# Softplus sum moved to TensorE, five GpSimd readouts and a reordered step-product store in a two-layer selective-scan kernel

## The chip, the cores and the metric

One core of a Trainium2 chip runs the whole program in one launch. The metric is device time in microseconds, median of several runs; lower is better. Engines are named TensorE (PE), VectorE (DVE), ScalarE (ACT), GpSimd (POOL) and SyncE (SP, which issues the DMAs).

## The reference

Two layers, each a selective scan ("mamba") followed by a mixture of experts. The change touches only the scan. For each of 4 sequences of 2305 positions:

```python
u = silu(conv4(u) + conv_b)                       # u, z = in_proj(seq)
dt = softplus(dt_raw @ dt_proj_w.T + dt_proj_b)
A = -exp(A_log)                                   # 128 channels x 16 states
def step(h, (dt_t, B_t, C_t, u_t)):
    dA = exp(dt_t[:, :, None] * A)
    h = dA * h + (dt_t * u_t)[:, :, None] * B_t[:, None, :]
    return h, einsum('bdn,bn->bd', h, C_t)
y = (ys + u * D) * silu(z)
out = y @ out_proj_w.T
```

## The kernel before, in words

A sequence is cut into 5 chunks of TC = 462 positions, so a layer runs NCH = 20 chunks one after the other, and the program runs 40. The 128 x 16 channel-state pairs make ITEMS = 16 tiles of 128 partitions, the items 0 to 15 of a chunk. For an item:

- GpSimd makes `dbu` (L689), the product of a row of dt times u and a row of B, in 4 buffers;
- ScalarE makes the decay exp(dt A) (L621) into one of 5 PSUM banks `state`;
- VectorE scans (`tensor_tensor_scan`). For items in ON_DVE the result stays in the bank (L811) and VectorE multiplies it by C into `hc` (L797), two neighbours in one instruction where it can; L795 copies the last column to `carry`. For items in ON_POOL the scan writes `last` (L808) and GpSimd multiplies it by C into `hcp` (L684). These multiplications are the readouts;
- TensorE sums the readouts into `ysum` with selection matrices (L504, L509).

A bank can be refilled when its scan (ON_POOL) or its readout (ON_DVE) is done. VectorE gates chunk k-1's sum with silu(z) (`gate`, L775) after item 2 of chunk k.

Beside the items of chunk k runs the front of chunk k+2: TensorE projects u, z (L446 to L451), then dt and B, C (L456, L460) into two PSUM banks `front`; ScalarE takes Silu (L550, L551), then for softplus Abs, Relu, Exp (L557 to L560), 1+e (L564), Ln (L568). `prep_rr` on VectorE (L714) makes a rounding remainder `rr`, `prep_ln` (L720) subtracts it from the Ln, `prep_dt` (L726) adds the Relu part and gives dt in `dd`. GpSimd's `prep` (L649) makes dt times u, here called the step product. SyncE stores B, C (`store_bc`, L338) and dt, dt times u (`store_dt`, four DMAs, L344) to DRAM and loads them back replicated over partitions into `rep` (`replicate_bc`, L351; `replicate_dt`, L359; four DMAs of 462 KB each). `rep` has two halves, one for each parity of chunks. Chunk k waits on `rep_loaded` for its half.

SyncE, like every engine, runs its list in order; in the loop of chunk k it holds: replicate_bc(k+1), store_dt(k+1), replicate_dt(k+1), load_xs(k+3), store_bc(k+2). The first of these waits for the last readout of chunk k-1. The front of chunks 0 and 1 is made ahead of the loop, between the tiles of the input's normalisation; here it is called the prologue.

Of the kernel before, what the change touches and what calls it, by code (L numbers as in the profile page):

```python
# [14 lines left out]
ALU = mybir.AluOpType  # L15
# [28 lines left out]
ON_POOL = (0, 3, 6, 8, 11, 13)  # L44
# [202 lines left out]
def phase_mamba(nc, a, g, l):  # L247
# [4 lines left out]
    with ExitStack() as ctx:  # L252
# [3 lines left out]
        u, sz = sb("u", [P, UBUFS, TC]), sb("sz", [P, UBUFS, TC])  # L256
        ab, ex, rx, rr = sb("ab", [P, TC]), sb("ex", [P, TC]), sb("rx", [P, TC]), sb("rr", [P, TC])
# [21 lines left out]
        xs_loaded, rep_loaded, bc_stored, dt_stored = sem("xs_loaded"), sem("rep_loaded"), sem("bc_stored"), sem("dt_stored")  # L279
# [28 lines left out]
        RESTS = NCH - 3 + (3 if l == 0 else 0)  # L308
# [3 lines left out]
        def chunk_of(eng, tile, k):  # L312

            if isinstance(k, int):
                return tile[:, k % UBUFS, :]
            return tile[:, bass.ds(eng.snap(k % UBUFS), 1), :]

        @block.sync
        def _(sp):
# [119 lines left out]
        def _(pe):  # L439
# [10 lines left out]
            def prep_z(k):  # L450
# [1356 lines left out]
```

## Time and profile before

| | before |
|---|---|
| median of 3 runs | 1935.14 us (1932.81 to 1940.75) |
| profiled execution | 1938.45 us, of which the span on the core is 1936.7 us |
| busy in the span | PE 1546.9, DVE 1271.6, POOL 1211.5, ACT 991.2 us |

The profile counts an engine busy while an instruction of its own runs; neighbouring instructions overlap by about 0.1 us, so the distance from one start to the next is what an instruction costs. Idle time is put down to the releaser whose event came last. Times in rows are microseconds from the start of the span.

### The profile page before, as it was taken

Reading aid. Unit: us, or ns where it says so; the run is one execution under the profiler, and the core shown is the slowest. Engines: PE = TensorE matmul, PEld = TensorE weight load, DVE = VectorE, ACT = ScalarE, POOL = GpSimd, SP = SyncE. Lnnn points to the kernel's source line nnn. Section 1 sums busy time; section 2 is a strip of 40 time slices with the busy share of each in tenths; the row PEclk is TensorE's granted clock in tenths of the full one; section 3 lists DMA queues with packets and bytes.
Section 4 is the critical chain, followed back from the end, with each engine's and each line's share of the span. In section 5 each row is a group of like instructions: output and inputs, shape, how many; then the busy total and the mean of one; then the engine's idle time right before and its main releaser. Section 6 shows DMA issues by size and latency. Waiting matters only on the chain. (4 is left out here: it accounts for less than half of the span.)

```text
span 1936.7 us, 25492 instructions
## 1 busy us (share of the span) xinstructions
PE 1546.9 (80%) x6220; PEld 927.2 (48%) x6221; DVE 1271.6 (66%) x2146; ACT 991.2 (51%) x1594; POOL 1211.5 (63%) x1179
## 2 busy tenths in 40 slices
PE   5677777777778998999982687777777777699996
PEld 3222222222228998989981222222222227566664
DVE  5799999999996531111115799999999996411012
ACT  4777777777772211222223777777777772122112
POOL 2699999999981001444435699999999992123310
PEclk8799999999995899999995799999999995599997
DMA  5788777787774204777765877788877881423313
GB/s 131 191 183 185 181 179 177 176 186 179 178 160 155 85 25 143 233 220 218 226 162 134 206 179 176 179 182 179 181 176 174 184 186 49 171 78 122 123 62 107
DMA packets 104507, 311.06 MB, mean 161 GB/s; under 512 B 19389, under 2 KB 74509, under 8 KB 93069
## 3 DMA queue, kind: packets, MB, share of 16 engines
q1 hardware_dynamic: 91896, 291.72, 60.1%
q0 software_dynamic: 12544, 18.63, 4.1%
q8 instruction: 20, 0.33, 0.1%
q14 instruction: 47, 0.38, 0.1%
HBM read 258.83 MB, written 51.45 MB: 160 GB/s over the span
## 5 line engine op out<-in xcount | busy, mean ns | idle before, releaser
L689 POOL TENSOR_TENSOR mamba_dbu<-mamba_rep 128x462 f32<-128x462 f32 x640 | 677.2, 1085 | 66.1 <-DMA mamba_rep<-dt_rows 66.1
L509 PE MATMUL mamba_ysum<-mamba_hc,all_sel 128*128 128x462 f32 x800 | 379.4, 588 | 148.3 <-DVE mamba_hc L797 147.3
L621 ACT ACTIVATE mamba_state<-mamba_rep,all_m_acol 128x462 f32<-128x462 f32 x640 | 388.9, 638 | 156.6 <-DVE mamba_last L808 155.6
L811 DVE TENSOR_TENSOR_SCAN mamba_state<-mamba_state,mamba_carry,mamba_dbu 128x462 f32<-128x462 f32 x400 | 455.4, 1179 | 0.0
L509 PEld LDWEIGHTS mamba_ysum<-mamba_hc,all_sel 128*128 128x128 f32 x800 | 130.3, 190 | 398.3 <-DVE mamba_hc L797 318.8
L808 DVE TENSOR_TENSOR_SCAN mamba_last<-mamba_state,mamba_last,mamba_dbu 128x462 f32<-128x462 f32 x240 | 280.3, 1168 | 15.2 <-POOL mamba_dbu L689 12.4
L684 POOL TENSOR_TENSOR mamba_hcp<-mamba_last,mamba_rep 128x462 f32<-128x462 f32 x240 | 266.7, 1111 | 5.6 <-DVE mamba_last L808 5.6
L504 PE MATMUL mamba_ysum<-mamba_hcp,all_sel 128*128 128x462 f32 x480 | 227.8, 570 | 50.1 <-POOL mamba_hcp L684 50.0
L797 DVE TENSOR_TENSOR mamba_hc<-mamba_state,mamba_rep 128x462 f32<-128x462 f32 (+1 forms) x240 | 230.7, 961 | 0.0
L1433 DVE TENSOR_TENSOR moe_h<-moe_sg,moe_up 128x512 f32<-128x512 f32 x62 | 42.6, 688 | 283.0 <-PE moe_up L1242 276.6
L504 PEld LDWEIGHTS mamba_ysum<-mamba_hcp,all_sel 128*128 128x128 f32 x480 | 85.3, 190 | 172.4 <-POOL mamba_hcp L684 119.6
L621 ACT ACT_TABLE_LOAD x80 | 102.6, 1283 | 103.6 <-DMA mamba_rep<-dt_rows 102.7
L1203 POOL DMA_INDIRECT token_rows<-moe_eo,moe_row x44 | 69.8, 1586 | 133.4 <-ACT moe_eo L1376 122.8
L1188 POOL DMA_INDIRECT moe_xs<-normed_rows,moe_row x44 | 43.5, 989 | 150.8 <-DVEq L1524 82.6
L1682 POOL DMA_INDIRECT last_rows<-experts_eo,all_row x32 | 31.5, 984 | 152.5 <-DVE experts_eo L1657 152.5
L1633 ACT ACTIVATE experts_hT<-experts_hid,weights_b 128x432 f32<-128x432 f32 x64 | 39.6, 620 | 156.0 <-PE experts_hid L1607 151.4
L1284 PE MATMUL moe_down<-weights_wd,moe_h 128*128 (+1 forms) x496 | 117.4, 380 | 0.8 <-ACT moe_eo L1376 0.8
L1616 PE MATMUL experts_down<-weights_w,experts_hT 128*108 128x256 f32 x512 | 112.5, 380 | 1.3 <-ACT experts_hT L1633 0.7
L1616 PEld LDWEIGHTS experts_down<-weights_w,experts_hT 128*108 128x108 f32 x512 | 87.9, 173 | 24.5 <-ACT experts_hT L1633 1.9
L1607 PE MATMUL experts_hid<-experts_xT,weights_w 128*128 128x432 f32 x256 | 96.3, 535 | 1.1 <-issue 1.1
L1284 PEld LDWEIGHTS moe_down<-weights_wd,moe_h 128*128 128x128 f32 x496 | 89.5, 190 | 10.8 <-issue 1.2
L1376 ACT ACTIVATE moe_eo<-moe_down,moe_weight 128x256 f32<-128x256 f32 x44 | 20.8, 473 | 135.7 <-PE moe_down L1284 135.7
(236 smaller groups left out, 2285.6 us busy)
## 6 DMA issues: line engine op xcount, KB each, us to landing
mamba_rep<-bc_rows SPq DMA_DIRECT2D x168, 462.0 KB, 7.4
mamba_rep<-dt_rows SPq DMA_DIRECT2D x168, 462.0 KB, 7.5
weights_wgu<-in_L_gu_dram SPq DMA_DIRECT2D x88, 512.0 KB
dt_rows<-mamba_dd SPq DMA_DIRECT2D x168, 115.5 KB, 7.2
weights_w<-in_L_w_dram SPq DMA_DIRECT2D x16, 1024.0 KB
mamba_xs<-seq_scratch SPq DMA_DIRECT2D x92, 116.0 KB, 9.2
seq_scratch<-mamba_y SPq DMA_DIRECT2D x40, 116.2 KB, 7.0
normed_rows<-xn SPq DMA_DIRECT2D x16, 288.0 KB, 7.1
```

Source lines behind the costliest of these rows:

```text
L504: nc.tensor.matmul(ysum[:, 0:TC], sel[:, i // NM, :], hcp[:, n % HCP, :], start=False, stop=end).then_inc(hcp_summed, 1)
L509: nc.tensor.matmul(ysum[:, 0:TC], sel[:, i // NM, :], hc[:, n % HCD, :], start=False, stop=end).then_inc(hc_summed, 1)
L621: nc.scalar.activation(state[:, STATE_BANK[i], 0:TC], rep[:, par * REP_ROWS + i // NM, :], ACT.Exp, scale=m["acol"][:, i:i + 1]).then_inc( ...
L684: pool.tensor_tensor(hcp[:, n % HCP, :], last[:, n, :], rep[:, first + 3 * NG + i % NM, :], ALU.mult).then_inc(hcp_ready, 1)
L689: pool.tensor_tensor(dbu[:, i % 4, :], rep[:, first + NG + i // NM, :], rep[:, first + 2 * NG + i % NM, :], ALU.mult).then_inc(dbu_ready, 1)
L797: nc.vector.tensor_tensor(hc[:, n % HCD:n % HCD + width, :], state[:, bank:bank + width, 0:TC], rep[:, c_rows + i % NM:c_rows + i % NM + w ...
L808: nc.vector.tensor_tensor_scan(last[:, n, :], bank, dbu[:, i % 4, :], last[:, n, TC - 1:TC], ALU.mult, ALU.add).then_inc(scan_done, 1)
L811: nc.vector.tensor_tensor_scan(bank, bank, dbu[:, i % 4, :], carry[:, i:i + 1], ALU.mult, ALU.add).then_inc(scan_done, 1)
L1203: pool.indirect_dma_start(out=g["to"][r % 2][:, :], out_offset=bass.IndirectOffsetOnAxis(ap=row[:, r:r + 1], axis=0), in_=eo[:, r % 2, :], ...
L1284: mm = nc.tensor.matmul(down[:, 0:C], h[:, par, f * P:(f + 1) * P], weights, start=(f == 0), stop=(f == FC0 - 1), skip_group_check=True)
L1607: mm = nc.tensor.matmul(hid[:, f % 2, 0:CAP], w1[:, par, k, f * P:(f + 1) * P], xT[:, par, k, :], start=(k == 0), stop=(k == 1))
L1616: mm = nc.tensor.matmul(down[0:CT, i % 2, 0:C], hT[:, f, i * CT:(i + 1) * CT], w2[:, par, f, :], start=(f == 0), stop=(f == FC1 - 1))
```

## The change

- `prep_ln` and `prep_dt` leave VectorE. ScalarE's Ln goes to `ab` in SBUF; TensorE adds `ab` + `rx` - `rr` with three matmuls (identity, identity, and `nident`, its negative) into the second `front` bank (`prep_add`); ScalarE copies the sum to `dd` (`prep_dd`).
- ON_POOL has five items, not six: (1, 4, 7, 10, 13). VectorE reads out eleven. Items 11 and 12 take C rows 3 and 0 and can't share an instruction. `hcp` has 5 buffers, `hc` 7.
- ScalarE's Silu for chunk k+2 stands behind decay 3 (it stood behind decay 6), Ln behind decay 12 (it stood behind 15), the new copy behind decay 15.
- GpSimd's step product for k+2 stands at the end of chunk k; it stood behind dbu 3 of chunk k+1.
- TensorE projects u and z one chunk earlier, for k+3 inside chunk k, and z waits for all of ScalarE's work on k+2. In SyncE's list store_dt(k+2) stands ahead of the wait for that z. `dt_rows` has two halves.
- `replicate_dt` counts on a semaphore of its own, `step_loaded`: ScalarE waits on it alone, VectorE on `rep_loaded` alone, GpSimd on both.
- The loops of SyncE, TensorE and ScalarE are written out, where they were loops with a register.

```diff
-ON_POOL = (0, 3, 6, 8, 11, 13)
+ON_POOL = (1, 4, 7, 10, 13)
-HCP = 3
-HCD = 5
-AT_SILU, AT_EXP, AT_ONE, AT_LN, AT_BC, AT_DT, AT_DTU, AT_Y, AT_RR = 6, 10, 11, 15, 13, 3, 3, 2, 13
+HCP = 5
+HC_SLOT = (0, 1, 2, 3, 4, 5, 6, 1, 2, 3, 4)
+AT_SILU, AT_EXP, AT_ONE, AT_BC, AT_LN, AT_U, AT_DTU, AT_Y, AT_RR, AT_ADD, AT_DD = 3, 6, 7, 8, 12, 9, 1, 2, 8, 7, 15
...
-            with sp.Fori(0, NCH) as k:
+            for k in range(NCH):
                 sp.wait_ge(decay_ready, items_before)
                 sp.wait_ge(dbu_ready, items_before)
+                sp.wait_ge(rep_loaded, replicas_before)
+                sp.wait_ge(step_loaded, replicas_before)
+                replicate_dt(k + 1)
                 sp.wait_ge(hc_ready, START + ND * k)
                 sp.wait_ge(hcp_ready, START + NP_ * k)
-                sp.wait_ge(rep_loaded, replicas_before)
                 replicate_bc(k + 1)
-                store_dt(k + 1)
-                replicate_dt(k + 1)
-                sp.wait_ge(front_mm, START + MMS * (k + 2) + MM_Z)
-                load_xs(k + 3)
                 store_bc(k + 2)
+                store_dt(k + 2)
+                sp.wait_ge(front_mm, START + MMS * (k + 3) + MM_Z)
+                load_xs(k + 4)
...
             def prep_z(k):
+                pe.wait_ge(front_act, START + ACTS * k)
...
+            def prep_add(k):
+                pe.wait_ge(front_act, START + ACTS * k + A_LN)
+                nc.tensor.matmul(front[:, 1, 0:TC], g["ident"][:, :], ab[:, :], start=True, stop=False)
+                nc.tensor.matmul(front[:, 1, 0:TC], g["ident"][:, :], rx[:, :], start=False, stop=False)
+                pe.wait_ge(front_dve, START + DVES * k + D_R)
+                nc.tensor.matmul(front[:, 1, 0:TC], nident[:, :], rr[:, :], start=False, stop=True).then_inc(front_mm, 1)
...
                 if s == AT_U1:
+                    pe.wait_ge(minus_ready, 1)
+                    prep_add(0)
                     prep_u(1)
                     prep_z(1)
...
-            def prep_ln(k):
-                nc.vector.tensor_tensor(front[:, 1, 0:TC], front[:, 1, 0:TC], rr[:, :], ALU.subtract).then_inc(front_dve, 1)
-            def prep_dt(k):
-                nc.vector.tensor_tensor(dd[:, 0, :], front[:, 1, 0:TC], rx[:, :], ALU.add).then_inc(front_dve, 1)
+            def prep_dd(k):
+                act.wait_ge(front_mm, START + MMS * k + MM_ADD)
+                nc.scalar.activation(dd[:, 0, :], front[:, 1, 0:TC], ACT.Copy).then_inc(front_act, 1)
```

Three places show how instructions move. The first is VectorE across the end of a chunk and the start of the next, before; `mamba_last` is what the scan of an ON_POOL item writes, `mamba_state` the PSUM banks.

```order
L811 SCALAR_TENSOR_TENSOR mamba_state<-mamba_state,mamba_carry,mamba_dbu 128x462 [waits mamba0_dbu_ready,mamba0_decay_ready] x2
L720 TENSOR_TENSOR mamba_front<-mamba_front,mamba_rr 128x462 [waits mamba0_front_dve,mamba0_front_act]
L795 COPY mamba_carry<-mamba_state 128x2 [waits mamba0_scan_done]
L797 TENSOR_TENSOR mamba_hc<-mamba_state,mamba_rep 128x924 [waits mamba0_hc_summed]
L726 TENSOR_TENSOR mamba_dd<-mamba_front,mamba_rx 128x462 [waits mamba0_front_dve,mamba0_dt_stored]
L808 SCALAR_TENSOR_TENSOR mamba_last<-mamba_state,mamba_last,mamba_dbu 128x462 [waits mamba0_dbu_ready,mamba0_decay_ready,mamba0_hcp_ready,mamba0_rep_loaded,mamba0_carry_zeroed]
```

The same place in the changed kernel, from the readout of items 11 and 12 to the scan of item 4 of the next chunk:

```order
L798 TENSOR_TENSOR mamba_hc<-mamba_state,mamba_rep 128x462
L813 SCALAR_TENSOR_TENSOR mamba_state<-mamba_state,mamba_carry,mamba_dbu 128x462 [waits mamba0_dbu_ready,mamba0_decay_ready] x2
L794 COPY mamba_carry<-mamba_state 128x2 [waits mamba0_scan_done]
L798 TENSOR_TENSOR mamba_hc<-mamba_state,mamba_rep 128x924 [waits mamba0_hc_summed]
L813 SCALAR_TENSOR_TENSOR mamba_state<-mamba_state,mamba_carry,mamba_dbu 128x462 [waits mamba0_decay_ready,mamba0_dbu_ready,mamba0_rep_loaded,mamba0_carry_zeroed]
L810 SCALAR_TENSOR_TENSOR mamba_last<-mamba_state,mamba_last,mamba_dbu 128x462 [waits mamba0_hcp_ready,mamba0_dbu_ready,mamba0_decay_ready]
L794 COPY mamba_carry<-mamba_state 128x1 [waits mamba0_scan_done]
L798 TENSOR_TENSOR mamba_hc<-mamba_state,mamba_rep 128x462 [waits mamba0_hc_summed]
L813 SCALAR_TENSOR_TENSOR mamba_state<-mamba_state,mamba_carry,mamba_dbu 128x462 [waits mamba0_dbu_ready,mamba0_decay_ready]
L774 TENSOR_TENSOR mamba_y<-mamba_ysum,mamba_sz 128x462 [waits mamba0_hcp_summed,mamba0_hc_summed]
L813 SCALAR_TENSOR_TENSOR mamba_state<-mamba_state,mamba_carry,mamba_dbu 128x462 [waits mamba0_dbu_ready,mamba0_decay_ready]
L810 SCALAR_TENSOR_TENSOR mamba_last<-mamba_state,mamba_last,mamba_dbu 128x462 [waits mamba0_hcp_ready,mamba0_dbu_ready,mamba0_decay_ready]
```

L720 and L726 are gone, and the carry copy that waits for the last scan stands right behind it, with nothing between.

The second is ScalarE over the first five decays of a chunk, in the changed kernel (before, the Silu pair stood behind the seventh):

```order
L630 ACTIVATE mamba_state<-mamba_rep,all_m_acol 128x462 [waits mamba0_hc_ready,mamba0_step_loaded]
L630 ACTIVATE mamba_state<-mamba_rep,all_m_acol 128x462 [waits mamba0_scan_done]
L630 ACTIVATE mamba_state<-mamba_rep,all_m_acol 128x462 [waits mamba0_hc_ready] x2
L551 ACT_TABLE_LOAD [waits mamba0_y_ready]
L551 ACTIVATE mamba_u<-mamba_front,all_m_vec 128x462 [waits mamba0_front_mm]
L552 ACTIVATE mamba_sz<-mamba_front 128x462
L630 ACT_TABLE_LOAD
L630 ACTIVATE mamba_state<-mamba_rep,all_m_acol 128x462 [waits mamba0_scan_done]
```

Decays 2 and 3 take the banks that items 14 and 15 of the chunk before held, and two table loads and both Silus now stand between decay 3 and decay 4.

The third is SyncE in one chunk of the changed kernel:

```order
L352 DMA mamba_rep<-dt_rows 32x3696 [waits mamba0_step_loaded,mamba0_rep_loaded,mamba0_dt_stored,mamba0_dbu_ready,mamba0_decay_ready]
L352 DMA mamba_rep<-dt_rows 32x3696 x3
L344 DMA mamba_rep<-bc_rows 32x3696 [waits mamba0_bc_stored,mamba0_hcp_ready,mamba0_hc_ready]
L344 DMA mamba_rep<-bc_rows 32x3696 x3
L330 DMA bc_rows<-mamba_bc 32x462 [waits mamba0_front_act]
L337 DMA dt_rows<-mamba_dd 64x1x462 [waits mamba0_front_pool]
L337 DMA dt_rows<-mamba_dd 64x1x462 x3
L322 DMA mamba_xs<-seq_scratch 64x464 [waits mamba0_front_mm]
L322 DMA mamba_xs<-seq_scratch 64x464
```

Both replications now follow each other, and the stores of the next step product come last but one.

## Rows read from the trace of the kernel before

**Rows 1.** Windows, gate to gate: length, busy (instructions) PE PEld DVE ACT POOL, clock, DMA, GB/s.

```profile
73.30:554.90 481.60, 372.76 (x835) 139.57 (x836) 475.06 (x615) 357.56 (x532) 457.39 (x437) 1.00 0.79 180
1095.80:1579.00 483.20, 373.82 (x836) 139.93 (x836) 474.73 (x615) 357.56 (x532) 457.10 (x437) 0.99 0.80 179
```

**Rows 2.** Waits in the first of these windows: total us, times, longest.

```profile
DVE mamba_last L808 <- POOL mamba_dbu L689: 4.8, 10, 0.8
...
POOL mamba_dbu L689 <- DMA mamba_rep<-dt_rows: 23.7, 19, 2.5
```

**Rows 3.** Timeline of VectorE in one chunk: start, length, instruction.

```profile
335.08 1.16 DVE L808 TENSOR_TENSOR_SCAN mamba_last<-mamba_state,mamba_last,mamba_dbu 128x462 f32<-128x462 f32 x1
336.15 0.14 DVE L795 COPY mamba_carry<-mamba_state 128x1 f32<-128x1 f32 x1
336.20 0.64 DVE L797 TENSOR_TENSOR mamba_hc<-mamba_state,mamba_rep 128x462 f32<-128x462 f32 x1
336.75 2.26 DVE L811 TENSOR_TENSOR_SCAN mamba_state<-mamba_state,mamba_carry,mamba_dbu 128x462 f32<-128x462 f32 x2
...
346.50 0.64 DVE L720 TENSOR_TENSOR mamba_front<-mamba_front,mamba_rr 128x462 f32<-128x462 f32 x1
347.03 0.17 DVE L795 COPY mamba_carry<-mamba_state 128x2 f32<-128x2 f32 x1
347.10 1.12 DVE L797 TENSOR_TENSOR mamba_hc<-mamba_state,mamba_rep 128x924 f32<-128x924 f32 x1
348.13 0.65 DVE L726 TENSOR_TENSOR mamba_dd<-mamba_front,mamba_rx 128x462 f32<-128x462 f32 x1
348.74 1.18 DVE L808 TENSOR_TENSOR_SCAN mamba_last<-mamba_state,mamba_last,mamba_dbu 128x462 f32<-128x462 f32 x1
...
351.97 0.62 DVE L775 TENSOR_TENSOR mamba_y<-mamba_ysum,mamba_sz 128x462 f32<-128x462 f32 x1
352.51 1.17 DVE L808 TENSOR_TENSOR_SCAN mamba_last<-mamba_state,mamba_last,mamba_dbu 128x462 f32<-128x462 f32 x1
```

**Rows 4.** Timeline of VectorE in the prologue: the second needs the first's result.

```profile
60.10 0.65 DVE L720 TENSOR_TENSOR mamba_front<-mamba_front,mamba_rr 128x462 f32<-128x462 f32 x1
60.85 0.64 DVE L726 TENSOR_TENSOR mamba_dd<-mamba_front,mamba_rx 128x462 f32<-128x462 f32 x1
```

**Rows 5.** Timeline of ScalarE: from Silu's table load to the next decays; two decays.

```profile
329.41 1.28 ACT L550 ACT_TABLE_LOAD   x1
...
333.10 2.36 ACT L621 ACTIVATE mamba_state<-mamba_rep,all_m_acol 128x462 f32<-128x462 f32 x4
...
341.18 1.22 ACT L621 ACTIVATE mamba_state<-mamba_rep,all_m_acol 128x462 f32<-128x462 f32 x2
```

**Rows 6.** Timeline of TensorE in a chunk: projections, two records to a matmul.

```profile
349.93 0.94 PE L446 MATMUL mamba_front<-mamba_xs,all_m_wu 128*128 128x462 f32 x2
350.71 0.94 PE L447 MATMUL mamba_front<-mamba_xs,all_m_wu 128*128 128x462 f32 x2
```

**Rows 7.** DMA issues of SyncE in one chunk.

```profile
351.94 2.59 SPq L344 DMA_DIRECT2D dt_rows<-mamba_dd  x4
360.84 1.72 SPq L359 DMA_DIRECT2D mamba_rep<-dt_rows  x4
```

**Rows 8.** Us to landing (last number): a store behind replicas; a store alone.

```profile
dt_rows<-mamba_dd SPq DMA_DIRECT2D x1, 115.5 KB, 6.8
...
seq_scratch<-mamba_y SPq DMA_DIRECT2D x1, 116.2 KB, 2.4
```

**Rows 9.** Timelines of the prologues: TensorE, then VectorE in layer 0 and layer 1.

```profile
43.62 1.75 PE L447 MATMUL mamba_front<-mamba_xs,all_m_wu 128*128 128x462 f32 x2
45.16 1.75 PE L451 MATMUL mamba_front<-mamba_xs,all_m_wz 128*128 128x462 f32 x2
...
70.08 1.18 DVE L808 TENSOR_TENSOR_SCAN mamba_last<-mamba_state,mamba_last,mamba_dbu 128x462 f32<-128x462 f32 x1
...
1091.35 0.44 DVE L777 MEMSET mamba_ysum<- 128x462 f32 x1 [10.64 <-DMA seq_scratch<-mamba_y]
```

More of the change, by code:

```diff
@@ L54 @@
 SUM_ORDER = tuple(sorted(range(ITEMS), key=lambda i: LAST_OF[i] + 2 if i in ON_DVE else i + 3.1))
-HCP = 3
-HCD = 5
-AT_SILU, AT_EXP, AT_ONE, AT_LN, AT_BC, AT_DT, AT_DTU, AT_Y, AT_RR = 6, 10, 11, 15, 13, 3, 3, 2, 13
+HCP = 5
+HC_SLOT = (0, 1, 2, 3, 4, 5, 6, 1, 2, 3, 4)
+HC_GAP = tuple(min(d for d in range(1, ND + 1) if HC_SLOT[n - d] == HC_SLOT[n]) for n in range(ND))
+HCD = max(HC_SLOT) + 1
+AT_SILU, AT_EXP, AT_ONE, AT_BC, AT_LN, AT_U, AT_DTU, AT_Y, AT_RR, AT_ADD, AT_DD = 3, 6, 7, 8, 12, 9, 1, 2, 8, 7, 15
 START = 16
@@ L372, in _ @@
                 sp.wait_ge(zeroed, 1)
-                for k in range(NCH, NCH + 3):
+                for k in range(NCH, NCH + 4):
                     sp.dma_start(g["seq"][k], hc[0:DM, :, :].rearrange("p n c -> p (n c)")[:, 0:CW]).then_inc(seq_rest, 16)
-            replicas = sp.alloc_register(f"replicas{l}")
             sp.wait_ge(padded, 3)
@@ L403, in _ @@
                     store_seq(b, c)
+            store_dt(1)
             sp.wait_ge(seq_rest, 16 * RESTS)
+            sp.wait_ge(front_mm, START + MMS * 2 + MM_Z)
+            load_xs(3)
             tiles["room_free"](sp)
-            with sp.Fori(0, NCH) as k:
-                sp.reg_mul(replicas, k, 16 * REPS)
-                sp.reg_add(replicas, replicas, 16 * REPS)
-                replicas_before = sp.snap(replicas)
+            for k in range(NCH):
+                replicas_before = 16 * NS * (k + 1)
                 items_before = START + ITEMS * k
@@ L492, in _ @@
                 tiles["tensor_weights"](pe, 1)
-            with pe.Fori(0, NCH) as k:
-                prep_u(k + 2)
-                prep_z(k + 2)
+            prep_add(1)
+            prep_u(2)
+            prep_z(2)
+            for k in range(NCH):
+                prep_dt(k + 2)
+                prep_bc(k + 2)
                 pe.wait_ge(y_ready, START + k)
-                nc.tensor.matmul(ysum[:, 0:TC], m["diag"][:, :], chunk_of(pe, u, k), start=True, stop=False)
+                nc.tensor.matmul(ysum[:, 0:TC], m["diag"][:, :], chunk_of(u, k), start=True, stop=False)
                 for at, i in enumerate(SUM_ORDER):
@@ L508, in _ @@
                         pe.wait_ge(hc_ready, START + ND * k + n + 1)
-                        nc.tensor.matmul(ysum[:, 0:TC], sel[:, i // NM, :], hc[:, n % HCD, :],
+                        nc.tensor.matmul(ysum[:, 0:TC], sel[:, i // NM, :], hc[:, HC_SLOT[n], :],
                                          start=False, stop=end).then_inc(hc_summed, 1)
-                    if at == AT_DT:
-                        prep_dt(k + 2)
-                    if at == AT_DT + 1:
-                        prep_bc(k + 2)
+                    if at == AT_ADD:
+                        prep_add(k + 2)
+                    if at == AT_U:
+                        prep_u(k + 3)
+                        prep_z(k + 3)
             pe.wait_ge(front_dve, START + DVES * (NCH + 2))
@@ L607, in _ @@
             nc.scalar.preload_act_table_set("exp_and_others")
-            with act.Fori(0, NCH // 2) as pair:
+            for pair in range(NCH // 2):
                 for par in range(2):
                     k = pair * 2 + par
-                    act.wait_ge(rep_loaded, 16 * REPS * (k + 1))
+                    act.wait_ge(step_loaded, 16 * NS * (k + 1))
                     for i in range(ITEMS):
```

106 lines of the change are left out of this document (49 added, 57 removed).

## The prediction

> **What bounds the kernel now.** I read three views in this order: the windows over each layer's chunks, who waits for whom inside them, and the timeline of one chunk. The windows show what fills a chunk. From the gate of chunk 0 to that of chunk 19 are 19 chunks: 481.6 / 19 = 25.35 us a chunk in layer 0 and 483.2 / 19 = 25.43 in layer 1, mean 25.39 [rows 1]. VectorE is busy 475.06 / 19 = 25.00 us of it, GpSimd 24.07, TensorE 19.62, ScalarE 18.82 [rows 1]. VectorE is the bound with 0.34 to 0.45 us idle a chunk. The waits say why it idles: 4.8 us in 19 chunks are for GpSimd's dbu, and GpSimd itself sat 23.7 us in 19 waits, 1.25 us each, for the replicas of dt [rows 2]. So there is a second loop just short of the bound: last readout, replicate_bc, store_dt, replicate_dt, first dbu. 40 of these chunks are some 1015 us of 1936.7. TensorE's granted clock there is 1.00 and 0.99 [rows 1], the level of 2.4 GHz.
>
> **VectorE's own work in a chunk** (start to start). Leaving: L720, 347.03 - 346.50 = 0.53, and L726, 348.74 - 348.13 = 0.61 [rows 3]. Coming: one more readout. Of eleven, 8 go in 4 double instructions as now, 3 go single (item 0, and 11 and 12 apart) where now 2 do, so one single of 336.75 - 336.20 = 0.55 [rows 3]. Six carry copies stay six; a scan into a bank and one into `last` both cost some 1.08. Work: 25.00 - 1.14 + 0.55 = 24.41 us.
>
> **What VectorE newly waits for.** First, the carry copy of items 14 and 15 now comes right behind the scan that it needs. Before, L720 stood between. An independent successor starts 0.09 us before its predecessor ends (335.08 + 1.16 against 336.15) [rows 3]; L726, which needed L720, began 0.10 after its end (60.10 + 0.65 against 60.85) [rows 4]. That is up to 0.19; other such pairs are not in my rows, and I take 0.16, with 0 to 0.25 as bounds.
> Second, decay 4. Count from the start of the readout of 14 and 15. It is over at 1.12 [rows 3] and frees the banks of decays 2 and 3. ScalarE then needs 1.22 for the two, 333.10 - 329.41 = 3.69 from Silu's table load to the next decay, and 2.36 / 4, about 0.64 with its tail, for decay 4 [rows 5]. With 0.07 for two hand-offs (an estimate; the bounds are 0 and the 0.10 of [rows 4] twice) it is ready at 6.75. VectorE would begin scan 4 at 1.03 (readout) + 4 x 1.08 (scans 0 to 3) + 0.05 + 0.55 (readout 0) + 0.54 (gate, 352.51 - 351.97) = 6.49 [rows 3]. It waits 0.26 to 0.30, every chunk; I take 0.29. Before, Silu came three decays later and had cover. Bounds: 0, if decay 2 gets away earlier, and 0.6.
> Third, what is left of today's idle: 0.07 (the sequence starts). The wait for GpSimd, 4.8 / 19 = 0.25 in layer 0 [rows 2], goes, if the next parts hold.
> New chunk: 24.41 + 0.16 + 0.29 + 0.07 = 24.93 us, against 25.39: 0.46 less, times 40 = 18 us.
>
> **GpSimd.** It does 22 multiplications, not 23, at 24.07 / 23 = 1.05 us [rows 1]: 23.0 us. Its readout of item 13 can begin 3.4 us before the last double readout (scans 14 and 15, one copy, the two singles lie between), the step product follows, so dbu 0 of the next chunk is done 0.2 us before the origin above, needed at 1.03. Cover 1.2 us.
>
> **TensorE.** 3 more matmuls at 350.71 - 349.93 = 0.78 [rows 6]: 19.6 + 2.3 = 22 us of 24.9. They hide in its waits for readouts. Ln ends near 16.4 us (decay 12 follows the readout of 5 and 6, then two table loads), the sum is there at 19.0, ScalarE copies by 20.1, behind decay 15 at 19.5; then z goes. Behind z's wait are queued the sums of items 10 to 15, which end at about 3.0 of the next chunk, the gate wants them at 4.9. Cover 1.9 us; without it each us late is a us a chunk. ScalarE gains one copy of about 0.55 and is at 19.4 of 24.9.
>
> **DMA and SyncE.** The step product now ends at -1.2 us. Four stores are issued in 2.6 us [rows 7], the last lands 2.4 us after its issue if nothing lies ahead, 6.8 behind replicas [rows 8]. The queue is empty there, so I take 2.4: SyncE, which has issued load_xs meanwhile, can replicate dt at 3.4, and behind it B and C. DMA work is 0.79 x 25.35 = 20.0 us a chunk [rows 1]; by bytes (8 x 462 KB of 8 x 462 + 4 x 115.5 + 2 x 116 + 58) the eight replicas are 16.7 of it. With 2.4 for start and landing and 0.3 for a bc store they are in at 22.8; VectorE loses nothing up to 24.9. Cover 2.1 us. The bc replication, today behind the last readout and first in the list, moves past dt's; both have the half free by then.
> The Trainium skill, DMA: Bandwidth & Descriptors, on the path of one DMA, puts most of a fixed cost of about 2 us on the write receipt and says that it "can cause a surprisingly long delay especially when the write target is HBM". The lone store agrees with its usual figure; its long case is the fourth rival.
>
> **The prologues**, which the change lengthens. Outside the loop nothing hides the addition: TensorE runs there at 45.16 - 43.62 = 1.54 us a matmul, half speed [rows 9], so three cost 4.6. Layer 0: the first addition delays the remaining tiles by 4.6, less about 1.7 since VectorE no longer stops there for Ln (an estimate; 0 to 2.3): 2.9. The second stands ahead of ScalarE's last weights: 4.6 + 0.55 for the copy - 1.28 for a table load that falls away with the loop - 1.0 that ScalarE has in hand today: 2.9. The first scan moves from 70.08 [rows 9] to about 75.9: 5.8 us. Layer 1: the first scan hangs on the stored sequence with VectorE idle 10.64 us until 1091.35 [rows 9], so much of the same 2.9 + 2.9 is covered; I take 2 (0 to 5). Together 7.8 (4 to 11).
> Behind the loop two of the saved VectorE instructions lie in its wait for the last sum: nothing.
>
> **Sum.** 1938.45 - 18.4 + 7.8 = 1927.9 for the profiled execution. That one lies 0.17% above the median of 1935.14, so 1925 as a median.
>
> **Rivals**, as medians.
> 1. The forecast, 1915 to 1935: chance 0.48.
> 2. The two new waits are not there (decay 2 starts early enough, a dependent copy is free): another 0.45 x 40 = 18 us, 1907. For it: ScalarE is idle over 6 us a chunk. Against: decay 2's bank is the one just read. 0.15.
> 3. ScalarE or TensorE later than counted: the chain Ln, sum, copy, z, item 10 has five hand-offs, and Silu with its loads has none to spare. A further 0.25 us a chunk gives 1935. 0.17.
> 4. The opposite side: the stores. If their landing takes 6.8 us without a queue too, the replicas are in at 22.8 + 4.4 = 27.2, 2.3 late. A step product made in chunk k feeds chunk k+2, so that is paid once in two chunks: 1.15 a chunk, 24.93 + 1.15 = 26.1, 40 x 0.7 = 28 slower, and the prologue: about 1970. It decides from 2.4 + 2.1 = 4.5 us on; halfway beyond it the time is some 1945. Against it: the lone store. 0.10.
> 5. The change doesn't do what it says: VectorE stays at 25.4, since it meets GpSimd or the code, now three times as long on TensorE, is late; only the prologue shows, 1943. 0.10.
>
> **From cases to numbers.** What differs by less than 0.5%, 9.7 us, this measurement hardly tells from no change; that bound is 1925.5 and the forecast sits on it. Faster: all of 2, somewhat over half of 1, a little of 3: 0.46. Same: the rest of 1, 3 and most of 5: 0.38. Slower: 4 and part of 5: 0.16. The range runs from 1908, at the edge of case 2, to 1946, which takes in 3, 5 and the near half of 4; case 1 alone is 1915 to 1935.
>
> **What would show it.** Gate to gate 24.9 us; VectorE busy 24.4 to 24.5; a wait of VectorE for decay 4 of near 0.3 in every chunk; no wait of GpSimd or ScalarE for replicas; last dt store landed in under 3 us; first scans near 76 and 1095. Wrong if GpSimd still waits for bc replicas (case 4), if the gate waits for `ysum` (case 3), or if the first scans come as early as before.

## The result, and the profile after

The changed kernel takes 1925.49 us (median of 5 runs, 1922.10 to 1929.57) against 1939.33 for the kernel before (median of 5 runs beside it; the 3 runs known at the time of the prediction gave 1935.14): ratio 0.9941, interval 0.9922 to 0.9959. The forecast was 1925.0. Beside the experiments the kernel before was timed again, with medians of 1940.12 (e1 to e4), 1939.66 (e5 to e8) and 1934.67 (e9 to e12), so kernels of different groups are compared by ratio. The profiled execution took 1925.49 us, its span 1923.7.

Windows of the kernel after, gate of chunk 0 to gate of chunk 19, layer 0 and layer 1, to be read against [rows 1]:

```profile
77.00:549.10 472.10, 400.65 (x951) 168.83 (x951) 468.12 (x597) 367.23 (x553) 432.43 (x419) 0.98 0.84 183
1093.30:1565.00 471.70, 400.62 (x950) 168.53 (x949) 468.07 (x597) 365.98 (x552) 432.82 (x419) 0.98 0.85 184
```

A chunk takes 472.1 / 19 = 24.85 and 24.83 us, where it took 25.35 and 25.43. Each layer's first gate is later on its own clock, though: 77.0 against 73.3 in layer 0, and in layer 1 the gate stands 53.8 us behind the first load of x, against 50.8. Of both, 0.6 us is the place of the gate and no delay: the readout of item 0 now stands ahead of it (3.85 us from the first scan to the gate in layer 0, 3.24 before). For the second, SyncE's issue of that load, before and after, and the gates' 1095.80 and 1093.30 of the windows:

```profile
1045.05 1.12 SPq L323 DMA_DIRECT2D mamba_xs<-seq_scratch  x2
```

```profile
1039.55 1.10 SPq L322 DMA_DIRECT2D mamba_xs<-seq_scratch  x2
```

Waits inside the first window, against [rows 2]. VectorE's wait for GpSimd and GpSimd's for the replicas of dt are gone; a wait for a decay is new:

```profile
DVE mamba_last L810 <- ACT mamba_state L630: 3.2, 16, 0.3
...
POOL mamba_dbu L702 <- DMA mamba_rep<-bc_rows: 1.0, 2, 0.8
```

VectorE in one chunk, against [rows 3]. The carry copy begins after the end of the scans (343.13 + 2.24 = 345.37), and the scan of item 4 waits 0.18 us for its decay:

```profile
343.13 2.24 DVE L813 TENSOR_TENSOR_SCAN mamba_state<-mamba_state,mamba_carry,mamba_dbu 128x462 f32<-128x462 f32 x2
345.41 0.16 DVE L794 COPY mamba_carry<-mamba_state 128x2 f32<-128x2 f32 x1
...
352.26 1.18 DVE L810 TENSOR_TENSOR_SCAN mamba_last<-mamba_state,mamba_last,mamba_dbu 128x462 f32<-128x462 f32 x1 [0.18 <-ACT mamba_state L630]
```

The DMA part of the page (last number: us to landing). A step store lands in 2.3 us, the lone store's 2.4 of [rows 8]; before it was 7.2:

```profile
dt_rows<-mamba_dd SPq DMA_DIRECT2D x176, 115.5 KB, 2.3
```

### The profile page after: what moved, and what is told of

The parts are those of the page before. It is cut to its first block and busy times, and to the rows that moved or that the text cites. A ratio compares the mean times of both kernels' runs of the same rounds, so it can differ in the third digit from the quotient of the medians.

```text
span 1923.7 us, 22854 instructions
## 1 busy us (share of the span) xinstructions
PE 1617.1 (84%) x6496; PEld 995.0 (52%) x6497; DVE 1250.0 (65%) x2100; ACT 1012.7 (53%) x1637; POOL 1158.8 (60%) x1141
## 5 line engine op out<-in xcount | busy, mean ns | idle before, releaser
L813 DVE TENSOR_TENSOR_SCAN mamba_state<-mamba_state,mamba_carry,mamba_dbu 128x462 f32<-128x462 f32 x440 | 504.8, 1172 | 0.7 <-ACT mamba_state L630 0.4
L517 PE MATMUL mamba_ysum<-mamba_hc,all_sel 128*128 128x462 f32 x880 | 392.4, 565 | 55.1 <-DVE mamba_hc L798 54.1
L517 PEld LDWEIGHTS mamba_ysum<-mamba_hc,all_sel 128*128 128x128 f32 x880 | 159.9, 191 | 261.1 <-issue 133.5
L798 DVE TENSOR_TENSOR mamba_hc<-mamba_state,mamba_rep 128x924 f32<-128x924 f32 (+1 forms) x280 | 250.0, 905 | 0.0
L810 DVE TENSOR_TENSOR_SCAN mamba_last<-mamba_state,mamba_last,mamba_dbu 128x462 f32<-128x462 f32 x200 | 231.6, 1158 | 6.4 <-ACT mamba_state L630 6.3
L697 POOL TENSOR_TENSOR mamba_hcp<-mamba_last,mamba_rep 128x462 f32<-128x462 f32 x200 | 200.8, 1004 | 40.7 <-DVE mamba_last L810 39.2
L512 PE MATMUL mamba_ysum<-mamba_hcp,all_sel 128*128 128x462 f32 x400 | 187.7, 551 | 0.0
L512 PEld LDWEIGHTS mamba_ysum<-mamba_hcp,all_sel 128*128 128x128 f32 x400 | 76.2, 190 | 80.0 <-issue 79.5
L453 PE MATMUL mamba_front<-mamba_u,all_m_wdt 128*128 128x462 f32 x88 | 49.1, 642 | 80.3 <-ACT mamba_sz L552 80.3
L1616 PEld LDWEIGHTS experts_down<-weights_w,experts_hT 128*108 128x108 f32 x512 | 87.9, 173 | 24.5 <-ACT experts_hT L1633 1.9
```

What stands on the lines that cost most here:

```text
L512: nc.tensor.matmul(ysum[:, 0:TC], sel[:, i // NM, :], hcp[:, n % HCP, :], start=False, stop=end).then_inc(hcp_summed, 1)
L517: nc.tensor.matmul(ysum[:, 0:TC], sel[:, i // NM, :], hc[:, HC_SLOT[n], :], start=False, stop=end).then_inc(hc_summed, 1)
L697: pool.tensor_tensor(hcp[:, n % HCP, :], last[:, n, :], rep[:, first + 3 * NG + i % NM, :], ALU.mult).then_inc(hcp_ready, 1)
L798: nc.vector.tensor_tensor(hc[:, HC_SLOT[n + w]:HC_SLOT[n + w] + at_once, :], state[:, bank + w:bank + w + at_once, 0:TC], rep[:, c_rows + ...
L810: nc.vector.tensor_tensor_scan(last[:, n, :], bank, dbu[:, i % 4, :], last[:, n, TC - 1:TC], ALU.mult, ALU.add).then_inc(scan_done, 1)
L813: nc.vector.tensor_tensor_scan(bank, bank, dbu[:, i % 4, :], carry[:, i:i + 1], ALU.mult, ALU.add).then_inc(scan_done, 1)
```

## Experiments

Twelve kernels, each profiled and timed against the kernel before. "Chunk" is gate 0 to gate 19 over 19, in layer 0 and layer 1. The stretch between the two layers' chunks, where most instructions are the same in all of them, differs from one profiled execution to the next (462 to 473 us), so mechanisms are read from chunks and gates, and time from ratios.

| kernel | chunk, us | ratio, interval |
|---|---|---|
| before | 25.35, 25.43 | 1 |
| after | 24.85, 24.83 | 0.9941 (0.9922 to 0.9959) |
| e1 old SyncE order | 25.02, 25.16 | 1.0002 (0.9990 to 1.0014) |
| e2 one matmul | 24.82, 24.82 | 0.9922 (0.9909 to 0.9935) |
| e3 Silu later | 24.57, 24.57 | 0.9898 (0.9884 to 0.9912) |
| e4 sum on VectorE | 25.93, 25.92 | 1.0128 (1.0111 to 1.0145) |
| e5 e3 + readout later | 24.45, 24.44 | 0.9862 (0.9840 to 0.9884) |
| e6 six readouts | 24.52, 24.53 | 0.9864 (0.9844 to 0.9885) |
| e7 prologue sum on VectorE | 24.83, 24.84 | 0.9924 (0.9907 to 0.9940) |
| e8 before, loops written out | 25.10, 25.16 | 0.9953 (0.9936 to 0.9970) |
| e9 e7 + store later | 24.83, 24.85 | 0.9932 (0.9919 to 0.9946) |
| e10 e5 + e9 | 24.43, 24.44 | 0.9860 (0.9843 to 0.9878) |
| e11 e6 + e9 + readout later | 24.46, 24.44 | 0.9873 (0.9854 to 0.9891) |
| e12 before, SyncE's loop written out | 25.07, 25.07 | 0.9943 (0.9927 to 0.9959) |

### e1: the old SyncE order in the kernel after

```diff
-                replicate_dt(k + 1)
                 sp.wait_ge(hc_ready, START + ND * k)
                 sp.wait_ge(hcp_ready, START + NP_ * k)
                 replicate_bc(k + 1)
-                store_bc(k + 2)
-                store_dt(k + 2)
+                if k > 0:
+                    store_dt(k + 1)
+                replicate_dt(k + 1)
                 sp.wait_ge(front_mm, START + MMS * (k + 3) + MM_Z)
                 load_xs(k + 4)
+                store_bc(k + 2)
+            store_dt(NCH + 1)
```

> The kernel after, with SyncE's issues in a chunk put back as they were: replicas of b and c, then the step stores, then the step replicas, then z's wait and the load of x, then the store of b and c. My theory: the stores queue behind the 14 us replicas again and land in about 7 us instead of 2.3, but the step replicas still end some 1.6 us before they are needed (2.1 before the change, less the 0.5 us by which a chunk is shorter), so the loops stay at 24.85 us a chunk and the time at 1925, within 4. Rival: the DMA chain binds, VectorE and ScalarE wait for step replicas at each chunk's start by 0.2 to 0.4 us: 1933 to 1941.

Measured 1.0002: the whole gain in time is gone. The rival holds and my expectation was wrong, by a plain error: 2.1 us is the cover that the prediction worked out for the new order. The old one had none, since GpSimd waited 1.25 us a chunk in it [rows 2]. Timeline of ScalarE, its wait at the head of a chunk, and the page's landing of the step stores:

```profile
346.01 2.38 ACT L632 ACTIVATE mamba_state<-mamba_rep,all_m_acol 128x462 f32<-128x462 f32 x4 [4.77 <-DMA mamba_rep<-dt_rows]
```

```profile
dt_rows<-mamba_dd SPq DMA_DIRECT2D x176, 115.5 KB, 8.7
```

And its windows:

```profile
75.20:550.60 475.40, 406.19 (x951) 170.70 (x952) 468.15 (x597) 367.01 (x553) 429.23 (x418) 0.97 0.80 182
1099.70:1577.80 478.10, 406.83 (x950) 171.12 (x950) 467.71 (x597) 365.00 (x551) 428.99 (x418) 0.97 0.80 181
```

VectorE is busy 24.6 us a chunk as in the kernel after, yet the chunk stays at 25.0 to 25.2. That this is the period of SyncE's loop of stores and replicas is borne out by e12, where the order is the same, VectorE has its old work of 25.0 us, and the chunk is 25.07. With the old order in place, VectorE's saving turns into waiting, here for dbu, as GpSimd and ScalarE stand still at the head of a chunk (23.9 and 87.7 us in 19 chunks, ScalarE's for the replicas of dt):

```profile
DVE mamba_state L815 <- POOL mamba_dbu L704: 5.0, 10, 1.2
```

So 0.30 of the 0.55 us that the change takes off a chunk stays in e1, as much as the written-out loop brings alone in e12, and 0.25 goes. Against the kernel after, the longer chunks explain some 10 of the 12 us (0.61%) that e1 is slower. Against the kernel before, the chunks of both layers save 11 us in the profile, the longer prologues take back 3.7, and stretches that the edits don't touch are 7.9 longer; no run shows why.

### e2: one matmul for the sum

```diff
-                nc.tensor.matmul(front[:, 1, 0:TC], g["ident"][:, :], ab[:, :], start=True, stop=False)
-                nc.tensor.matmul(front[:, 1, 0:TC], g["ident"][:, :], rx[:, :], start=False, stop=False)
                 pe.wait_ge(front_dve, START + DVES * k + D_R)
-                nc.tensor.matmul(front[:, 1, 0:TC], nident[:, :], rr[:, :], start=False, stop=True).then_inc(front_mm, 1)
+                nc.tensor.matmul(front[:, 1, 0:TC], g["ident"][:, :], ab[:, :], start=True, stop=True).then_inc(front_mm, 1)
```

> The kernel after, with one matmul in place of the three in TensorE's sum: the ReLU part and the polynomial part are left out of the step size, so the output isn't the reference's. My theory: the three matmuls are free in the loops, where TensorE waits 1.8 us a chunk for Silu, and cost only on the dependent chain of the prologues: 2 matmuls less, three times at the slow 1.5 us in the first layer's prologue and at about 0.8 us in the second's; so 2 to 5 us less, 1922, and a chunk unchanged at 24.84. Rival: TensorE's position sets the step chain or the readout slots: 0.1 to 0.3 us off each chunk, 1914 to 1921, with the chunk at 24.55 to 24.75.

The chunk stays at 24.82: inside the loops the two matmuls that e2 leaves out are free. The third and ScalarE's copy were not tried alone. Layer 0's first gate comes at 74.6 and not 77.0, the 2 us expected of the prologue, but with the same prologue it came at 75.4 in e3 and 77.9 in e5, and the ratios' intervals overlap: what the two matmuls cost there isn't shown.

### e3: Silu and Exp one decay later

```diff
-AT_SILU, AT_EXP, AT_ONE, AT_BC, AT_LN, AT_U, AT_DTU, AT_Y, AT_RR, AT_ADD, AT_DD = 3, 6, 7, 8, 12, 9, 1, 2, 8, 7, 15
+AT_SILU, AT_EXP, AT_ONE, AT_BC, AT_LN, AT_U, AT_DTU, AT_Y, AT_RR, AT_ADD, AT_DD = 4, 7, 8, 9, 12, 9, 1, 2, 8, 7, 15
```

> The kernel after, with ScalarE's two Silus behind decay 4 instead of 3 and the Exp group behind decay 7 instead of 6. My theory: VectorE's wait of 0.18 us for decay 4 with the 0.10 us of lost overlap goes, and no other decay comes late, because the Exp group moves too: 0.28 us off each of 40 chunks, 11 us, 1914 (1911 to 1918). Rival: ScalarE is late by the same at the next decay that it does after a table load (decay 5 or 8), or TensorE, held 1.2 us longer at the Silu wait, gives back the readout slots late: 1925, 1923 to 1929.

24.84 - 24.57 = 0.27 us a chunk (expected: 0.28), and VectorE has no wait for a decay left. Four numbers in a list bring three quarters as much as the whole change (0.9898 against 0.9941). The 11 us appear as 0.43%, some 8 us, in the ratios, whose intervals allow both.

### e4: the sum back on VectorE

In part; the rest takes out TensorE's three matmuls and ScalarE's copy and does the same to the prologues:

```diff
...
+                        if i == 11:
+                            prep_ln(k + 2)
                         if i - 1 in ON_DVE and not FIRST[i - 1]:
                             read_out(i - 2 if SECOND[i - 1] else i - 1)
+                        if i == 13:
+                            prep_dt(k + 2)
...
```

> The kernel after, with the sum of the softplus parts back on VectorE as two additions behind scans 11 and 13 of a chunk (and in the prologues), and TensorE's three matmuls and ScalarE's copy taken out. Everything else stays, the store order and the five GpSimd readouts too. My theory: VectorE is the bound and has no hidden room, so each chunk grows by the two additions, 2 x 0.55 us = 1.1, so 24.84 to 25.95, 44 us in all, and the prologues give 3 to 6 us back: 1965 (1960 to 1971). Rival: ScalarE's and GpSimd's waits share the bound, so part of the additions hides in the 0.2 us idle and the 0.3 us of late decay 4: +0.6 to 0.8 a chunk, 1944 to 1952.

Measured 1966.6, the chunk 25.93: +1.08, both additions in full. Windows of layer 0:

```profile
76.10:568.70 492.60, 371.66 (x833) 153.82 (x833) 488.96 (x634) 355.53 (x530) 437.95 (x418) 0.95 0.81 175
```

VectorE's busy time grew by (488.96 - 468.12) / 19 = 1.10. So with the store order in, VectorE is the bound; e1 says that without it, it isn't.

### e5: the carry copy away from its scan

On top of e3's edit:

```diff
-                        if i - 1 in ON_DVE and not FIRST[i - 1]:
+                        if i - 1 in ON_DVE and not FIRST[i - 1] and i != 13:
                             read_out(i - 2 if SECOND[i - 1] else i - 1)
+                    read_out(11)
```

> The kernel of the later Silu (chunk 24.50 us, 1919.5), with one more move: the double readout of items 11 and 12 goes from behind scan 13 to behind scan 15, between that scan and the carry copy of items 14 and 15, which needs scan 15's result. My theory: the copy's exposed dependency of 0.13 us a chunk goes, 5 us in all: 24.37 us a chunk, 1914. Rival: ScalarE's decay 0, which writes the bank that this readout frees, starts 2.3 us later, and VectorE waits for it at the chunk's start, 0.1 to 0.5 us: 1918 to 1935.

24.57 - 24.44 = 0.13 a chunk and 1913.36 us. Both terms for which the prediction had new waits are now priced by themselves, and without them the windows give

```profile
77.90:542.40 464.50, 406.36 (x950) 174.75 (x950) 463.85 (x597) 364.35 (x552) 430.80 (x418) 0.95 0.85 186
```

24.45 us a chunk with VectorE idle for 0.03: the prediction's bare work was 24.41.

### e6: six readouts on GpSimd

```diff
-ON_POOL = (1, 4, 7, 10, 13)
+ON_POOL = (0, 3, 6, 8, 11, 13)
...
-HCP = 5
-HC_SLOT = (0, 1, 2, 3, 4, 5, 6, 1, 2, 3, 4)
+HCP = 3
+HC_SLOT = (0, 1, 2, 3, 4, 5, 6, 0, 1, 2)
```

> The kernel after, with six readouts on GpSimd at the items of the kernel before and ten on VectorE; the sum on TensorE and the store order stay. My theory: VectorE loses one single readout of 0.55 us and GpSimd comes to 22.8 + 1.0 = 23.8 us of a chunk, not yet the bound; some of the 0.55 is lost to waits for GpSimd, so 24.85 falls to 24.45, 16 us less, 1910 (1904 to 1918). Rival: GpSimd, without cover, takes its place as the bound together with the handing back of scans, at 24.8 us or more: 1925 to 1935.

```profile
74.70:540.60 465.90, 396.40 (x950) 168.39 (x950) 458.98 (x577) 367.33 (x552) 458.33 (x437) 0.99 0.85 186
```

24.52 a chunk and ratio 0.9864: going from six readouts to five, which the change does, costs 0.3 us a chunk with the rest in place. GpSimd (458.33 / 19 = 24.12) and VectorE (24.16) are then level. The 0.3 is the price of the whole list of items and not of a readout alone, since the scans' order and VectorE's waits for decays change with it (3.2 us in 16 waits in the kernel after, 2.4 in 10 here).

### e7 and e9: the prologues

e7 puts the sums of chunks 0 and 1 on VectorE; e9 has this edit besides:

```diff
-            store_dt(1)
             sp.wait_ge(seq_rest, 16 * RESTS)
+            store_dt(1)
```

> The kernel after, with the sum for chunks 0 and 1 alone, outside the loops, back on VectorE; the loops keep TensorE's. My theory: the two groups of three matmuls at half clock with their copies leave the prologues' chain: the first scan of the first layer goes from 73.1 to about 69.5 us, that of the second gains 1 to 3 us: 5 us less in all, 1920 (1917 to 1923). Rival: VectorE again stops for Ln in the first prologue and the second hangs on the stored sequence: 1 us or less, 1925.

> The kernel of the VectorE sum in the prologues, with the prologue's second group of step stores moved behind SyncE's wait for the stored sequence. In that run VectorE's first instruction after the prologue waited until 71.15 us for the sequence, 7.4 us after its last store was issued, against 4.6 us in the kernel before, and four step stores stood right behind it in the queue. My theory: those stores slow the sequence's landing. Moved, the sequence lands some 2.5 us sooner, the first scan of layer 0 begins at 69.5 to 70.5 and not at 72.3, and layer 1's likewise 2 us sooner: 1920 to 1921. Rival: the landing varies by itself or the replicas are the cause, the first scan stays at 72, 1925.

Timelines of SyncE and VectorE, e7, then e9. The first instruction behind the prologue waits for the sequence in both:

```profile
57.21 6.50 SPq L359 DMA_DIRECT2D seq_scratch<-mamba_y  x10
63.76 3.49 SPq L337 DMA_DIRECT2D dt_rows<-mamba_dd  x4
...
71.15 0.44 DVE L787 MEMSET mamba_ysum<- 128x462 f32 x1 [6.70 <-DMA seq_scratch<-mamba_y]
```

```profile
57.09 7.92 SPq L359 DMA_DIRECT2D seq_scratch<-mamba_y  x10
69.18 2.51 SPq L337 DMA_DIRECT2D dt_rows<-mamba_dd  x4
...
69.42 0.44 DVE L787 MEMSET mamba_ysum<- 128x462 f32 x1 [2.31 <-DMA seq_scratch<-mamba_y]
```

With four step stores right behind it, the sequence was in 71.15 - 63.71 = 7.4 us after its last issue, without them 69.42 - 65.01 = 4.4. The first scan began at 72.34 and 70.61, just outside the range of the theory. This is weaker than it looks. e9's last issue came 1.3 us later by itself; and e10, which has e9's order and nothing behind the sequence, took 6.7 us from the last issue. Counted from the first of the ten issues, the sequence took 13.9 us in e7 and 14.7 in e4, which both have step stores right behind it, and 11.9 to 13.2 in the six kernels without (before, e8 to e12); e2, with the stores 2 us behind, is between them at 13.7. The means differ by 1.7 us, so the theory is likely in layer 0, at less than the expected 2.5 us, and not shown by one pair of executions. In layer 1 nothing moved (47.9 and 47.8 us from the first load of x to that instruction), where I expected 2 us. By ratio e7, e9 and the kernel after can't be told apart, so the prologue's microseconds are seen in the profile alone.

### e8 and e12: the kernel before with loops written out

```diff
-            with sp.Fori(0, NCH) as k:
-                sp.reg_mul(replicas, k, 16 * REPS)
-                sp.reg_add(replicas, replicas, 16 * REPS)
-                replicas_before = sp.snap(replicas)
+            for k in range(NCH):
+                replicas_before = 16 * REPS * (k + 1)
```

That is e12; e8 does the same to TensorE's and ScalarE's loops too.

> The kernel before, with the loops of SyncE, TensorE and ScalarE over the chunks written out and nothing else changed. My theory: registers and branches lie in waits, so nothing but the table load behind the loop's head changes: 1939, within 3 (chunk 25.39). Rival: the loops' registers sit on the chain of SyncE's replicas that VectorE meets, and 0.1 to 0.3 us a chunk comes back: 1927 to 1935; or longer code fetches cost the same the other way, 1943 to 1950.

> The kernel before, with SyncE's loop over the chunks alone written out. With all three loops written out a chunk went from 25.28 to 25.03 us and the time to 1929.6. SyncE then issued the first replica of b and c 0.14 us after the readout that frees the rows, against 0.67 us in loop form. My theory: that half microsecond sits on the loop of stores and replicas that GpSimd waited for, so SyncE's loop gives most of it: chunk 25.03 to 25.12, 1930 to 1934. Rival: the gain is from TensorE's or ScalarE's loop (ScalarE's wait for the replicas at the chunk's head fell from 2.7 to 1.1 us): chunk 25.25, 1939.

For e8 I expected nothing and was wrong; e12's theory holds. e12's chunk is 25.07, 0.32 less than before, its ratio 0.9943, that of the whole change. Windows and waits of e12 in layer 0:

```profile
72.90:549.20 476.30, 372.51 (x836) 139.71 (x836) 474.59 (x615) 357.66 (x532) 457.25 (x437) 1.00 0.81 181
```

```profile
POOL mamba_dbu L687 <- DMA mamba_rep<-dt_rows: 18.5, 18, 2.1
...
DVE mamba_last L806 <- POOL mamba_dbu L687: 0.8, 2, 0.5
```

VectorE's work is untouched (474.59 / 19 = 24.98), its wait for GpSimd is down from 4.8 to 0.8 us [rows 2]. The half microsecond is seen at SyncE. In the kernel before, the readout that frees the rows ends at 372.07 + 1.12 = 373.19 and the replicas are issued 0.58 us later; in e12 it is 368.62 + 1.13 = 369.75 and 0.14. In 18 chunks of layer 0 it is 0.56 to 0.58 before and 0.13 to 0.15 in e12. The profile doesn't show the register instructions themselves; that they are the cause follows from the edit, which changes nothing else. First before, then e12:

```profile
372.07 1.12 DVE L797 TENSOR_TENSOR mamba_hc<-mamba_state,mamba_rep 128x924 f32<-128x924 f32 x1
...
373.77 1.96 SPq L351 DMA_DIRECT2D mamba_rep<-bc_rows  x4
```

```profile
368.62 1.13 DVE L795 TENSOR_TENSOR mamba_hc<-mamba_state,mamba_rep 128x924 f32<-128x924 f32 x1
...
369.89 1.70 SPq L351 DMA_DIRECT2D mamba_rep<-bc_rows  x4
```

e8's chunk is 25.10 and 25.16, so TensorE's and ScalarE's loops add nothing to this.

### e10 and e11: together

e10 is e5 with both prologue edits; e11 is e6 with them and with item 12's readout behind scan 15.

> The later Silu and Exp groups, the readout of 11 and 12 behind scan 15, the prologues' sum on VectorE and their second step stores behind the wait for the sequence, all on the kernel after. My theory: the gains lie in different places and add: chunk 24.38 as with the first two (1913.4), and 5 us of prologues: 1909 (1905 to 1913). Rival: the prologue part gives nothing, as in its first form: 1913.

> Six readouts on GpSimd (chunk 24.51, 1914.3), with the single readout of item 12 behind scan 15 and the two prologue edits, Silu where the change has it. GpSimd is busy 24.1 us of that chunk and VectorE 24.15. My theory: GpSimd is now level with VectorE, so of the 0.13 us dependency some 0.05 to 0.1 comes back: chunk 24.43, and 5 us of prologues, 1906 (1902 to 1911). Rival: GpSimd binds, the chunk stays at 24.5, and only the prologues show: 1909; or decay 0 is late and costs 0.2 a chunk, 1917.

Both chunks came out as expected (24.44 and 24.45). The time, 1906.4 and 1911.34 us beside 1934.67, is no better by ratio than e5's and e6's. The intervals of e5, e6, e10 and e11 overlap, so none of them is shown to be the best: they are 1.3 to 1.4% below the kernel before and 0.7 to 0.8% below the change. The 5 us that were expected of the prologues don't show in the ratios.

## Why the prediction was right, and where it was not

**The bound.** That VectorE was the bound with a second loop just behind it was right, and both halves matter: e4 shows the first in the new order, e1 the second in the old.

**VectorE's chunk.** The terms held one by one. The decay-4 wait was put at 0.29 and is 0.27 (e3); the exposed copy at 0.16 and is 0.13 (e5); the bare work at 24.41, and 24.44 is what is left without both; the chunk at 24.93 and is 24.84. Most of the difference is the "0.07 for what is left of today's idle". One sign was missed: VectorE was to be busy 24.4 to 24.5 us a chunk and is busy 24.64. It is 24.41 in e5: where an instruction must wait for the one before it or for a decay, the usual overlap of 0.09 us is lost, and the profile counts that as busy; this is most of the 0.23. 0.55 x 40 = 22 us came from the loops, taken at 40 chunks, where the sum had 18.4.

**Whose gain it is.** The prediction booked the 0.25 us a chunk of GpSimd's wait as a gain of the new store order and gave the written-out loops no term. e12 gets 0.32 a chunk, with the old order and VectorE's old work, from SyncE's loop alone. Against that kernel the rest of the change saves (25.07 - 24.84) x 40 = 9 us in the loops and pays some 6 in the prologues (first scan 73.11 against 69.61 us, and 49.9 against 47.2 from the first load of x in layer 1), and no difference is left in the ratios. The diff had the line and the profile had the loop; what I missed is that SyncE's register work lies on it. The total came out all the same, because both edits remove the same wait and it can go only once. The order still has a worth of its own: with the old one the chunk stays at 25.1 us even with VectorE's smaller work (e1).

**GpSimd.** Right in direction: its wait for dt's replicas is gone, and the one for those of B and C is 1.0 us in 19 chunks. It is busy 22.8 us, predicted 23.0. The page has five readouts a chunk at 1004 ns each; six took 1111.

```profile
L697 POOL TENSOR_TENSOR mamba_hcp<-mamba_last,mamba_rep 128x462 f32<-128x462 f32 x200 | 200.8, 1004 | 40.7 <-DVE mamba_last L810 39.2
```

**TensorE.** Predicted hidden, and hidden (for two of the three matmuls e2 shows it; VectorE has no wait for TensorE in the window); busy 21.1 us a chunk where the sum had 22.

**DMA.** The store's landing was predicted at 2.4 and is 2.3, so the fourth rival, and with it the long receipt of which the Trainium skill (DMA: Bandwidth & Descriptors, Anatomy of one DMA) warns, has no case here. The new order has cover for ScalarE and VectorE, which don't wait for replicas. But the 2.1 us were counted up to VectorE's need; GpSimd needs B's rows sooner, for its first dbu, and waits for them in 2 of 19 chunks. With shorter chunks this grows: 3.9 us in 9 waits in e5, 5.5 in 8 in e6. So the replicas look like the bound that comes next.

**The prologues.** The step with a wrong size is the first addition of layer 0. The layer was put at 5.8 and the first scan moved from 70.08 [rows 9] to 73.11, so 3.0. From one profiled execution to another this varies as much: with the new prologue the first scan began at 71.3 to 74.0 (after, e1, e3, e5, e6; mean 72.3), with the old one at 69.1 to 70.1 (before, e8, e12; mean 69.6). The second addition is as counted: ScalarE waits 4.62 us for TensorE and is paid for it with the table load.

```profile
68.70 0.56 ACT L575 ACTIVATE mamba_dd<-mamba_front 128x462 f32<-128x462 f32 x1 [4.62 <-PE mamba_front L461]
...
73.11 1.19 DVE L813 TENSOR_TENSOR_SCAN mamba_state<-mamba_state,mamba_carry,mamba_dbu 128x462 f32<-128x462 f32 x1 [0.41 <-ACT mamba_state L630]
```

The first addition was to cost 2.9 and cost nothing that is seen: the tiles' copies end at 64.09 instead of 63.77, on a timeline that was 0.6 late before it. TensorE's timeline says why. The addition takes the slow 1.6 us for two matmuls, the third is quicker, and the three projections behind it, which took 1.55 each before [rows 9], take 0.78. That gives back 2.3 of its 4.0 us, and the 1.7 left are as much as the prediction took off for VectorE's stop:

```profile
41.07 1.80 PE L458 MATMUL mamba_front<-mamba_ab,all_ident 128*128 128x462 f32 x2
42.66 1.75 PE L459 MATMUL mamba_front<-mamba_rx,all_ident 128*128 128x462 f32 x2
44.20 1.02 PE L461 MATMUL mamba_front<-mamba_rr,mamba_nident 128*128 128x462 f32 x2
45.06 0.94 PE L442 MATMUL mamba_front<-mamba_xs,all_m_wu 128*128 128x462 f32 x2
...
46.61 0.94 PE L448 MATMUL mamba_front<-mamba_xs,all_m_wz 128*128 128x462 f32 x2
```

Layer 1 was put at 2. Counted like layer 0, to the first scan, it is 1092.57 - 1045.05 = 47.5 us from the first load of x before and 1089.49 - 1039.55 = 49.9 after, so 2.4:

```profile
1092.57 1.18 DVE L808 TENSOR_TENSOR_SCAN mamba_last<-mamba_state,mamba_last,mamba_dbu 128x462 f32<-128x462 f32 x1
```

```profile
1089.49 1.19 DVE L813 TENSOR_TENSOR_SCAN mamba_state<-mamba_state,mamba_carry,mamba_dbu 128x462 f32<-128x462 f32 x1
```

**The total.** The prologues lose 5.4 us, predicted 7.8. From the first scan to the last gate the layers win 9.1 and 11.1, together 20.2, predicted 18.4. That is -14.7 for the part that the change touches; the other stretches are 1.7 longer, and the profiled executions differ by 13.0, predicted 10.6. The forecast of 1925.0 hit 1925.49 by half a microsecond, and that is luck: it took 10 us off a base of 1935.14, and the measured change is 14 off a base of 1939.33.

**Rivals.** The second (no new waits) is what e5 builds: predicted at 1907, which had the longer prologues in it. e5 measured 1913.36 beside 1939.66; its ratio of 0.9862 on the prediction's base of 1935.14 gives 1908. The third and the fifth would have shown as a wait for `ysum` or a chunk of 25.4; neither is there. Fifth in another shape, though: the gain of the order and the gain of the written-out loop are largely one gain.

## What to carry to other kernels

Where two loops of different engines have nearly the same period, price every edit on both, and ask which one a plain rewriting would free: here writing out the loop of a DMA queue was worth as much, on the old kernel, as the whole redesign. What the loop form would cost on the new one was not run. An instruction list's places are worth a scan of their own: moving Silu by one item and a readout by two brought 0.8% where the change had brought 0.6%. And when an expected gain depends on another engine's slack, undo one part at a time; undoing the sum's move costs 1.9%, undoing the order 0.6%, and undoing the five readouts gains 0.8%.

## What was not expected of the hardware

TensorE's granted clock, from windows of the prologue of layer 0, kernel before and kernel after (columns as in [rows 1]):

```profile
42.00:46.70 4.70, 4.70 (x8) 1.97 (x7) 0.36 (x2) 1.99 (x3) 0.00 (x0) 0.50 0.96 201
```

```profile
41.00:44.20 3.20, 3.20 (x6) 1.47 (x5) 0.42 (x1) 1.04 (x3) 0.00 (x0) 0.50 1.04 222
45.00:47.40 2.40, 2.40 (x8) 1.09 (x7) 0.00 (x0) 1.84 (x2) 1.16 (x1) 1.00 0.96 197
```

In the same place of the program it is 0.50 (1.2 GHz) before and, after three more matmuls without a pause, 1.00 (2.4 GHz): added work paid for 2.3 of its own 4.0 us. The other way round, in the chunks TensorE now stops for Silu, and the matmul behind the stop is slow; no wait of VectorE for TensorE comes of it, but it lowers the granted clock of the window to 0.98, and to 0.93 in e3, where it stops longer (71.4 us of weight loads waiting for Silu in 19 chunks, against 55.9). Kernel after:

```profile
350.32 1.04 PE L453 MATMUL mamba_front<-mamba_u,all_m_wdt 128*128 128x462 f32 x2 [1.84 <-ACT mamba_sz L552]
351.29 1.53 PE L464 MATMUL mamba_front<-mamba_u,all_m_wbc 128*32 128x462 f32 x2
```

A store that is issued later may delay earlier ones: with four step stores right behind it, the stored sequence of layer 0 landed some 1.7 us later, counted from its first issue (e7 and e4 against six kernels without). In layer 1 e7 and e9 show no such difference.
